# Routed experts of a two-layer gated block: weights split beforehand into DRAM scratch, and three float32r products in place of one float32 product

## The reference

```
x = x + tanh(g_xattn[0]) * attention_0(layernorm(x), ctx)
x = x + tanh(g_ffn[0])   * mixture_0(layernorm(x))
x = x + tanh(g_xattn[1]) * attention_1(layernorm(x), ctx)
x = x + tanh(g_ffn[1])   * mixture_1(layernorm(x))
```

## Time and profile before

| | |
|---|---|
| median of three runs | 2507.49 us (2500.48 to 2511.79) |
| the profiled execution, its own time | 2506.47 us |
| its span, first to last instruction | 2504.0 us |
| mean granted TensorE clock in it | 0.918 |
| PE / DVE / ACT / POOL busy | 84% / 43% / 29% / 30% |

### The profile page before, as it was taken

How to read it: one execution, slowest core, us unless ns; L and a number is a source line. 1 busy time by engine, 2 the same in 40 slices (tenths; PEclk the granted TensorE clock), 3 DMA queues, 4 the chain that set the end, 5 groups by cost and what they waited for, 6 DMA issues and landing times.

```text
span 2504.0 us, 37079 instructions
## 1 busy us (share of the span) xinstructions
PE 2107.5 (84%) x9370; PEld 1371.6 (55%) x9370; DVE 1067.8 (43%) x2507; ACT 732.8 (29%) x1105; POOL 747.2 (30%) x534
## 2 busy tenths in 40 slices
PE   5489799788837788888687887999979699999995
PEld 3267678444414555555566664555545356555663
DVE  6754543211128889888467632222212122222221
ACT  4541111122225766565511111222212122122221
POOL 0011000334435767574100102333322233233331
PEclk8699899899976998899889898999989899999998
DMA  3110010555562222220300045343454643434334
GB/s 111 63 66 27 0 51 34 176 93 99 94 149 45 47 36 36 38 40 1 119 27 26 1 172 157 68 83 65 99 164 92 190 90 65 112 66 69 65 69 97
DMA packets 95030, 194.25 MB, mean 78 GB/s; under 512 B 14778, under 2 KB 18746, under 8 KB 94779
## 3 DMA queue, kind: packets, MB, share of 16 engines
q0 software_dynamic: 33600, 79.73, 18.1%
q1 hardware_dynamic: 61242, 112.34, 15.0%
HBM read 943.63 MB, written 61.60 MB: 401 GB/s over the span
## 4 chain that ended last, share of the span: by engine, by line
PE 25%; SPq 17%; issue 5%; DVE 3%; DMA 1%; ACT 1%; POOL 0%; POOLq 0%; DVEq 0%; ACTq 0%
PE ps L1419 9%; PE ps L1441 6%; PE ps L1346 5%; SPq L1166 5%; PE ps L1364 2%; SPq L1162 2%; SPq L1147 2%; SPq L1148 1%; SPq L1149 1%; SPq L1150 1%; SPq L1169 1%; SPq L1151 1%; SPq L1152 1%; SPq L1154 1%; SPq L1156 1%
## 5 line engine op out<-in xcount | busy, mean ns | idle before, releaser
L1419 PE MATMUL ps<-f_wb,f_xT 128*128 x1776 | 564.0, 461 | 2.3 <-ACT f_xT L1267 2.3
L1441 PE MATMUL ps<-f_w2b,f_hT 128*128 x822 | 405.1, 628 | 97.8 <-issue 56.8
L1419 PEld LDWEIGHTS ps<-f_wb,f_xT 128*128 128x128 f32 x1776 | 330.2, 191 | 198.7 <-issue 58.3
L1530 POOL DMA_INDIRECT y_scratch<-f_yo,f_rows x150 | 237.6, 1584 | 441.8 <-ACT f_yo L1273 310.0
L1780 DVE TENSOR_TENSOR f_g<-ps,f_bb 128x352 f32<-128x352 f32 x111 | 58.3, 525 | 586.4 <-PE ps L1419 443.5
L1510 POOL DMA_INDIRECT f_xg<-xn_scratch,f_rows x150 | 159.7, 1064 | 441.1 <-PE ps L1403 220.6
L1441 PEld LDWEIGHTS ps<-f_w2b,f_hT 128*128 128x128 f32 x822 | 151.2, 199 | 244.7 <-issue 244.5
L586 POOL TENSOR_TENSOR a_elo<-a_e,a_ehi 128x768 f16<-128x768 f32 x128 | 218.8, 1719 | 137.5 <-ACT a_ehi L642 135.5
L1273 ACT ACTIVATE f_yo<-ps,f_share 128x512 f32<-128x512 f32 x150 | 103.1, 687 | 356.4 <-PE ps L1441 340.4
L818 DVE TENSOR_REDUCE a_nmax<-ps 128x1 f32<-128x512 f32 x256 | 163.9, 680 | 40.5 <-PE ps L673 40.3
L1346 PE MATMUL ps<-f_xhi,f_w13hi 128*128 128x512 f32 x448 | 175.5, 392 | 2.8 <-POOL f_w13lo L1485 2.8
(11 more groups left out here) (226 smaller groups left out, 3150.7 us busy)
## 6 DMA issues: line engine op xcount, KB each, us to landing
f_wb<-in_f_w_dram SPq DMA_DIRECT2D x216, 2816.0 KB
f_wb<-in_f_w_dram SPq DMA_DIRECT2D x72, 1536.0 KB
f_w2b<-in_f_w_dram SPq DMA_DIRECT2D x261, 256.0 KB
f_bb<-bias_scratch SPq DMA_DIRECT2D x111, 352.0 KB
f_w2b<-in_f_w_dram SPq DMA_DIRECT2D x111, 192.0 KB
f_wraw<-in_f_w_dram SPq DMA_DIRECT2D x14, 768.0 KB, 5.2
xn_scratch<-f_xn SPq DMA_DIRECT2D x32, 256.0 KB, 2.1
y_scratch<-x_res SPq DMA_DIRECT2D x8, 1024.0 KB, 5.3
```

The costliest lines, as they stand in the source:

```text
L1419: mm = pe.matmul(columns((UB if w else GB) + b % 2, H), xT[:, b % 2, k, :], weights(at, w, k), start=(k == 0), stop=(k == KD - 1))
L1441: mm = pe.matmul(ps[:, OB + b % 2, :], hT[:, b % 2, P * j:P * j + P], w2b[:, bass.ds(buf, 1), j, :].rearrange("p o d -> p (o d)"), start=( ...
L1530: pool.indirect_dma_start(y_d, bass.IndirectOffsetOnAxis(ap=rows_of[:, b:b + 1], axis=0), yo[:, b % 3, :], None, bounds_check=ROWS + P - 1 ...
```

## The change

The routed experts' weights are split before they are needed. There are 56 pieces (12 of layer 0, 44 of layer 1), each of 128 x 1536 floats: SP loads a piece (768 KB), one engine rounds it to float32r (`high`), POOL takes the rest (`low`), and SP stores both to DRAM scratch laid out by expert (`store`: 1 MB for W1 and W3, 0.5 MB for W2). Raw pieces and W1/W3 results have two buffers, the W2 result `self.down` has one. Sixteen pieces (`AT_ONCE`) are done in attention 0, `high` and `low` both on POOL. The other forty are done in mixture 0: six (`EARLY`) on POOL ahead of the shared part's first pair, and 34 spread over its 32 steps, with `high` on ACT and `low` on POOL. Attention 0 also writes zeros and the split W2 bias into the scratch of layer 1.

```
+        class Stage:
+            def load(self, sp, i, layer, chunk):
+                if i >= 2:
+                    sp.wait_ge(self.lo_done, i - 1)
+                sp.dma_start(self.raw[:, i % 2, :], a[f"f{layer}_w"][chunk, :, :]).then_inc(self.raw_in[i % 2], 16)
+            def high(self, eng, copy, i):
+                eng.wait_ge(self.raw_in[i % 2], 16 * (i // 2 + 1))
+                if i >= 2:
+                    eng.wait_ge(self.up_out[i % 2], 16 * (i // 2))
+                for w in range(2):
+                    copy(self.part(i, w, 0), self.source(i, w))
+                if i >= 1:
+                    eng.wait_ge(self.down_out, 16 * i)
+                copy(self.down[:, 0, :], self.raw[:, i % 2, 1024:1536]).then_inc(self.hi_done, 1)
+            def low(self, pool, i):
+                pool.wait_ge(self.hi_done, i + 1)
+                for w in range(2):
+                    pool.tensor_tensor(self.part(i, w, 1), self.source(i, w), flt(self.part(i, w, 0)), ALU.subtract)
+                pool.tensor_tensor(self.down[:, 1, :], self.raw[:, i % 2, 1024:1536], flt(self.down[:, 0, :]),
+                                   ALU.subtract).then_inc(self.lo_done, 1)
+            def store(self, sp, i, layer, chunk):
...
+                sp.wait_ge(self.lo_done, i + 1)
+                sp.dma_start(w13_d[layer][e0:e0 + 4, :, blk, :].rearrange("s p n -> p s n"),
+                             flt(self.up[:, i % 2, :, :])).then_inc(self.up_out[i % 2], 16)
+                r = blk % 4 * 32
+                sp.dma_start(w2_d[layer][e0:e0 + 4, r:r + 32, blk // 4, :],
+                             flt(self.down[:].rearrange("p h d -> p (h d)"))).then_inc(self.down_out, 16)
```

In attention 0 (SP, then POOL), and in mixture 0 (POOL, then ACT's shared part):

```
+                for e in range(E1):
+                    sp.dma_start(g["w2_d"][1][e, rest:P, HC1 - 1, :], zero[rest:P, :]).then_inc(zero_out, 16)
...
+                for i in range(AT_ONCE):
+                    stage.store(sp, i, *g["PREPARED"][i])
+                    if i + 2 < AT_ONCE:
+                        stage.load(sp, i + 2, *g["PREPARED"][i + 2])
...
+                for i in range(AT_ONCE):
+                    stage.high(pool, pool.tensor_copy, i)
+                    stage.low(pool, i)
...
+                if layer == 0:
+                    for i in range(EARLY):
+                        stage.high(pool, pool.tensor_copy, i)
+                        stage.low(pool, i)
...
+                    more(8 * p)
                     for t in range(1, B):
                         up(p, t)
+                        for s in ((8 * p + 1, 8 * p + 2), (8 * p + 3, 8 * p + 4),
+                                  (8 * p + 5, 8 * p + 6, 8 * p + 7))[t - 1]:
+                            more(s)
```

The fetches go by expert, through a ring of three experts in SBUF; `fetch(e)` is two or three loads (layer 0: 1.5 MB and 0.75 MB; layer 1: 2.9 MB, 1.6 MB and the biases, 0.4 MB). SP waits on the first block of expert e-2, from a table of the router's counts:

```
+                for e in range(3, E):
+                    begun = sp.value_load(first_of[0:1, e - 2:e - 1], min_val=1, max_val=BLOCKS)
+                    sp.wait_ge(d_mm, begun)
+                    sp.wait_ge(w_in, 16 * e * LOADS)
+                    fetch(e)
```

The products of the routed part on TensorE, the second half of the copies on ACT and DVE:

```
+                    for k in range(KD):
+                        for xt, low in ((xThi, 0), (xThi, 1), (xTlo, 0)):
+                            mm = pe.matmul(out, xt[:, b % 2, k, :], weights(at, w, k, low), start=(m == 0),
+                                           stop=(m == 3 * KD - 1))
...
+                    for j in range(HC):
+                        n = LAST_K if j == HC - 1 else P
+                        for ht, low in ((hThi, 0), (hThi, 1), (hTlo, 0)):
+                            mm = pe.matmul(ps[:, OB + b % 2, :], ht[0:n, b % 2, P * j:P * j + P],
...
+                def turned_back(b):
+                    act.wait_ge(hT_tr, b + 1)
+                    wait(act, d_mm, b - 1)
+                    act.copy(hThi[:, b % 2, :], ps[:, HB, 0:HC * P]).then_inc(hT_hi, 1)
...
+                def turned_rows(b):
+                    dve.wait_ge(xT_hi, b + 1)
+                    wait(dve, u_mm, b - 1)
+                    dve.tensor_tensor(xTlo[:, b % 2, :, :].rearrange("p k t -> p (k t)"), ps[:, XB, :],
+                                      flt(xThi[:, b % 2, :, :].rearrange("p k t -> p (k t)")),
+                                      ALU.subtract).then_inc(xT_lo, 1)
```

More of the change, by code:

```diff
@@ L36 @@
 ]
+for m in MOE:
+    m["NB"], m["HC"] = m["H"] // 32, -(-m["H"] // P)
+    m["chunks"] = 2 * m["NB"] * (m["E"] // 8)
+    m["size"] = 512 * m["NB"] + 1024 * m["HC"]
+AT_ONCE = 16
+EARLY = 6
 ROWS = NT * P
@@ L120, in build @@
+        PREPARED = [(0, c) for c in range(MOE[0]["chunks"])] + [(1, c) for c in range(MOE[1]["chunks"])]
         cross_attention_0(nc, a, sb, locals())
@@ L1069, in bank, with prepared, gated, piece @@
             return OB + i % 2
[L1071 to L1087, removed]
+        def prepared(step):
+            n0 = AT_ONCE + EARLY
+            left = len(g["PREPARED"]) - n0
+            return range(EARLY + left * step // STEPS, EARLY + left * (step + 1) // STEPS) if layer == 0 else ()
+        def gated(b, w):
+            return ps[:, GB + b % 2, 0:2 * H].rearrange("p (n j) -> p n j", j=64)[:, :, 32 * w:32 * w + 32]
+        def piece(i):
+            return g["PREPARED"][AT_ONCE + i]
         with nc.Block() as block:
@@ L1137, in keep @@
                                  x[:, TB * t:TB * t + TB, :]).then_inc(y_out, 16)
+                for s in range(STEPS):
+                    for i in prepared(s):
+                        stage.store(sp, i, *piece(i))
+                        if AT_ONCE + i + 2 < len(g["PREPARED"]):
+                            stage.load(sp, i + 2, *piece(i + 2))
+                    if s == 20:
+                        if BIASED:
+                            sp.wait_ge(brow_out, 16 * 2 * (E // 4))
+                        sp.wait_ge(cw_out, 16)
+                        sp.wait_ge(rows_ready, 1)
+                        sp.wait_ge(table_ready, 1)
+                        fetch(0)
                 keep(0)
@@ new lines, in _ @@
+                sp.wait_ge(w_in, 16 * 2 * LOADS)
+                fetch(2)
+                for e in range(3, E):
[3 more added lines that the diff above has]
+                    fetch(e)
+                if layer == 0:
+                    for i in range(2):
+                        sp.wait_ge(stage.up_out[i], 8 * (len(g["PREPARED"]) - AT_ONCE))
+                    sp.wait_ge(stage.down_out, 16 * (len(g["PREPARED"]) - AT_ONCE))
@@ L1224, in _, with more @@
                     act.activation(red[:], lg[:, :, E], ACT.Exp, scale=-1.0).then_inc(exp_done, 1)
+                def more(s):
+                    for i in prepared(s):
+                        stage.high(act, act.copy, i)
                 def up(p, t):
@@ L1400, in turned @@
                     rows_in(pe, b)
[L1401 removed]
+                    wait(pe, xT_lo, b)
                     for k in range(KD):
@@ L1507, in _ @@
                         pool.sem_inc(raw_free[h], 1)
+                    for s in range(8 * p, 8 * p + 8):
+                        for i in prepared(s):
+                            stage.low(pool, i)
                 def gather(b):
@@ L1684, in tables @@
+                    link(dve.tensor_scalar(third, e, 11, None, ALU.mult))
+                    link(dve.tensor_scalar(third, third, 5, None, ALU.logical_shift_right))
+                    link(dve.scalar_tensor_tensor(out=third_of, in0=third, scalar=-3.0, in1=e, op0=ALU.mult,
+                                                  op1=ALU.add))
+                    link(dve.tensor_scalar(at, third_of, SIZE, None, ALU.mult))
+                    link(dve.tensor_copy(first_of[:], start[0:1, :]))
                     dve.sem_inc(table_ready, 1)
```

341 lines of the change are left out of this document (156 added, 185 removed).

## The result

The changed kernel takes 2942.72 us (median of 4 runs, 2941.92 to 2953.95) where the one before takes 2508.18 beside it: a ratio of 1.175, 95% interval 1.171 to 1.179. The forecast was 2565 us with 2470 to 2690. The direction was right, the size was not: it is 434 us slower, not 58. The profiled execution has a span of 2940.9 us against 2504.0.

What follows compares the result with a forecast made beforehand. TensorE was taken to bound layer 1's routed part and layer 0's shared part, POOL's scatter chain layer 0's routed part; 94 + 138 + 0 - 177 + 3 = +58 us on 2506.5 gave 2565 us, range 2470 to 2690.

Steps and rivals of the forecast that it cites:

- The period of a piece: Weight preparation: cast, three POOL subtractions and two stores follow in turn through one `self.down` buffer, 10.9 us a piece.
- Attention 0, +94: Attention 0: fifteen piece periods and the last store end the stage at 201 us in place of 106.5, +94 us.
- Mixture 0, +138: Layer 0's prologue and shared part: forty pieces delay the first routed product from 347 to 487 us after stage start, +138.
- The four breaks: Mixture 0: the piece chain stops where ACT waits for a pair's first U, about 10 us each, 40 in all.
- Layer 1's routed part, -177: Layer 1's routed experts: float32r blocks of 6.75 us plus 55 us of stalls take 804 us instead of 981.
- Layer 0's routed part, 0: Layer 0's routed experts: the scatter chain stays at 5.6 us, so no net change, from -25 to +30 us.
- Rival 1: Layer 1's routed part: large fetch rows starve the scatters, 57 us more, 2613 us in all; chance 0.15.
- Rival 2: Layer 1's routed products: float32r at 352 columns costs as at 512, blocks of 8.25 us, 2692 us; chance 0.08.
- Rival 3: Preparation in attention 0 and mixture 0: stores land sooner, period 9.1 us, kernel faster at 2466 us; chance 0.20.
- Rival 4: Preparation does not bind: pieces overlap and POOL's 6.3 us a piece set the pace, 2312 us; chance 0.03.

## Why the prediction was wrong, by its own steps

- **The period of a piece: the step that failed.** "Half as much again at 371 GB/s adds 1.4, so 5.7 to 6.7; I take 5.9". The W2 store was priced as half of a 1 MB store, at the rate of 16 engines; it runs on four, and both stores take 13.2 us, +7.3. The other terms hold: cast 0.62 (0.61), subtractions 3.74 (4.05), handover 0.1 (0.3). The sum is 17.7 instead of 10.9, and my upper bound of 13.5 was too low for the same reason, since "8" for the stores was taken from full-width stores as well. 55 periods by 6.8 are 374 us, and the time missed by 378. The row that I took it from (a 1 MB store) has another pattern, and the destination `[4, 32, 1024]` stood in the diff. With the store split, the measured period is 10.99 and the time 2601, inside the range. So that the change costs time at all was rightly forecast by its mechanism, the chain through the single buffer.
- **Attention 0, +94.** About +210 as it was. With the split store the last piece is through POOL at 202.4, where the forecast had 195. The periods were right and the start wasn't: the first piece was 3 us earlier, and the second came 20.3 us after it instead of 10.9, behind the zero stores. POOL's 103 idle us of before did not cover the pieces, as forecast.
- **Mixture 0, +138.** About +407 as it was. With the split store the first routed product is at 723 against 688. The four breaks cost 13 to 14 us each instead of 10, and single pieces wait for their raw load (periods of 11.3 to 14.4). That the chain runs unbroken through both stages is shown by the run with eight pieces in attention 0.
- **Layer 1's routed part, -177.** Right: 964.8 to 787.4, -177.4. The timeline of PE shows one block of 6.75 us, gate product to gate product, with 0.163 us from matmul to matmul at 352 columns (0.160 taken):

```profile
2251.63 0.49 PE L1529 MATMUL ps<-f_wb,f_xThi 128*128 x2
2251.96 0.32 PE L1529 MATMUL ps<-f_wb,f_xTlo 128*128 x1
2252.12 0.48 PE L1529 MATMUL ps<-f_wb,f_xThi 128*128 x2
...
2258.38 0.49 PE L1529 MATMUL ps<-f_wb,f_xThi 128*128 x2
```

  The stalls are 787.4 - 110 x 6.75 = 45 us (55 taken), nearly all at experts of the middle: gaps of 11 to 19 us at seven blocks from the 38th to the 72nd. The gaps of 23 to 28 us that before had at three blocks are gone. By the N/2.4 + 2.5 ns of the Trainium skill, "TensorE: Matmul & The Clock Gate", section "Back-to-back issue gap", the matmul would be 149 ns; the trace has 163.
- **Layer 0's routed part, 0.** Right: 275 us against 273. The timeline of POOL has the scatters 5.7 us apart, each behind the landing of the one before:

```profile
1200.53 1.59 POOL L1631 DMA_INDIRECT y_scratch<-f_yo,f_rows  x1 [2.90 <-DMA y_scratch<-f_yo,f_rows]
1206.26 1.59 POOL L1631 DMA_INDIRECT y_scratch<-f_yo,f_rows  x1 [2.77 <-DMA y_scratch<-f_yo,f_rows]
```

- **The rivals.** None came in. Rival 1 would show in the stalls, which were under the forecast's, and the smaller rows changed them by 7 us. Rival 2 is excluded by 0.163 us. Rival 3 needed a period of 9.1 us, and even with the store split it is 10.99. Rival 4 needed a period of 6.3 us; the run with two buffers shows that even a second buffer gives 11.3 while four engines carry the store. What was missing is a rival on how many DMA engines the new store gets. It had a price in the rows: four engines of 16 at 371 GB/s move 93 GB/s, 5.7 us for the W2 part alone. With 4.3 for the up store before it and 2.1 for the raw load's rows (768 KB at 371 GB/s) on the same engines, an estimate of 12.1 us would have come out, against the 13.2 measured.

## What to carry over

A new DMA is priced by its pattern, not only by its bytes. Take its duration from a row with the same slowest dimension, and where there is none, divide the rate by the share of engines it will get: here four starts of 32 rows instead of one of 4 x 32 took 342 us off the kernel, and two starts of 2 x 32 added 223. Where a chain through one buffer repeats 55 times, every term of a period is worth 55 times its error, and an upper bound has to cover another mechanism too, not only a slower case of the same one. Send first what holds the single buffer: doing the W2 part first took another 119 us, and together with smaller changes it made a kernel 1.9% faster than the one before.

## What was not expected of the hardware

- Splitting a transfer can make it slower: two stores whose slowest dimension is two share the same two DMA engines (share 0.13), 22.3 us a piece instead of 17.7 with one store.
- A transfer on few engines delays all that share these engines: the raw load of 768 KB, on all 16, lands after 13.9 us behind it (9.1 to 17.7) and after 5.7 (4.9 to 11.2) with the store split.
- PE does its work for the shared part of layer 0 more slowly in a window in which it waits more than half the time: the granted clock is 0.72 instead of 0.96 over the window, and the busy time 296 us instead of 275 for the same number of matmuls within 1%.
